# Second attention: four points' stacks instead of two shared ones, and another order at a group's border

## The reference

```python
qkv = (x @ w_qkv.T + b_qkv)                     # 16 heads of 8
std_logits = einsum('bhqd,bhkd->bhqk', q, k) * scale
write_lines = exterior(x_prev @ w1_write.T, x @ w2_write.T)   # 6 numbers a head, unit length
read_lines = exterior(x @ w1_read.T, x @ w2_read.T)
incidence = einsum('bqhp,bkhp->bhqk', read_lines, write_lines @ J6)
bias = incidence * decay ** (q - k) * (k < q) * bias_scale
attn = softmax(causal(std_logits + bias))
out = attn @ v @ w_out.T + b_out
x = x + out
```

## Time and profile before

| | us |
|---|---|
| median of 3 runs | 1821.87 |
| lowest, highest run | 1816.07, 1834.79 |
| profiled execution, span | 1776.1 |
| TensorE busy in the span | 1455.7 (82%) |
| VectorE busy | 1274.7 (72%) |
| ScalarE busy | 935.2 (53%) |
| GpSimd busy | 694.1 (39%) |
| DMA queue of SP, share of 16 engines | 28.1% |

### The profile page before, as it was taken

The page is one execution under the profiler, slowest core; times in us unless marked ns, Lnnn a source line. Parts: engine busy times, 40 slices in busy tenths (PEclk is TensorE's granted clock), DMA queues, the critical chain, the costliest instruction groups (busy, mean ns, idle before and its releaser), DMA issues. The chain is left out here.

```text
span 1776.1 us, 37567 instructions
## 1 busy us (share of the span) xinstructions
PE 1455.7 (82%) x11726; PEld 964.8 (54%) x11726; DVE 1274.7 (72%) x3482; ACT 935.2 (53%) x1914; POOL 694.1 (39%) x812
## 2 busy tenths in 40 slices
PE   3999999999999729995378887878888887837993
PEld 1224334333343319994256766666666665627993
DVE  6777888888787435555777879697978786834555
ACT  2577777777775505662435455454545453314561
POOL 3122342633520334554233344444444541233552
PEclk8699999999998969997689999898999998978997
DMA  6211111111110332222544443434344434132225
GB/s 158 66 42 59 47 52 53 61 53 49 49 62 15 128 123 67 73 72 82 164 150 126 126 128 106 131 109 129 112 125 122 130 111 138 38 130 56 71 72 162
DMA packets 122418, 166.37 MB, mean 94 GB/s; under 512 B 21490, under 2 KB 96018, under 8 KB 121586
## 3 DMA queue, kind: packets, MB, share of 16 engines
q1 hardware_dynamic: 113330, 145.69, 28.1%
q0 software_dynamic: 8896, 18.30, 3.0%
HBM read 116.04 MB, written 47.60 MB: 92 GB/s over the span
## 5 line engine op out<-in xcount | busy, mean ns | idle before, releaser
L1124 DVE TENSOR_REDUCE a_M<-a_F 128x1 f32<-128x512 f32 x512 | 325.8, 683 | 90.0 <-PE a_F L1318 88.1
L1025 ACT ACTIVATE L_W<-a_ST 128x512 f32<-128x512 f32 x512 | 276.8, 595 | 89.1 <-PE a_ST L1359 88.3
L2028 ACT ACTIVATE L_W<-c_ST 128x1024 f32<-128x1024 f32 x160 | 163.3, 1021 | 188.4 <-PE c_ST L2408 141.1
L2630 ACT ACTIVATE L_hT<-L_P,L_W1s 128x128 f32<-128x128 f32 x600 | 171.5, 368 | 142.9 <-PE L_P L2711 110.6
L2616 POOL DMA_INDIRECT L_yd<-L_ys,L_di x150 | 163.1, 1087 | 151.6 <-DVE L_ys L2662 147.2
L489 POOL DMA_INDIRECT L_xd<-L_XN,L_place_i x128 | 124.4, 972 | 146.5 <-issue 131.9
L1359 PE MATMUL a_ST<-L_W 74*128 74x512 bf16 x512 | 168.9, 395 | 11.1 <-ACT L_W L1025 6.3
L1318 PE MATMUL a_F<-L_W 72*128 72x512 bf16 x512 | 167.1, 403 | 7.7 <-DVE a_M L1124 6.9
L2702 PE MATMUL L_P<-L_xT,L_W1s 128*128 128x128 f32 x1200 | 161.0, 278 | 0.0
L2711 PE MATMUL L_P<-L_W,L_hT 128*128 x1200 | 159.1, 276 | 0.1
L2407 PE MATMUL c_ST<-ident,c_SD 128*128 128x128 f32 x512 | 149.7, 292 | 5.5 <-ACT L_W L2028 5.5
(11 more groups left out here) (430 smaller groups left out, 3164.9 us busy)
## 6 DMA issues: line engine op xcount, KB each, us to landing
c_QS<-c_q SPq DMA_DIRECT2D x32, 504.0 KB
c_QS<-c_rd SPq DMA_DIRECT2D x32, 378.0 KB
L_xg<-L_xd SPq DMA_DIRECT2D x150, 64.5 KB
L_W<-a_q SPq DMA_DIRECT2D x32, 288.0 KB
L_W<-a_k SPq DMA_DIRECT2D x96, 96.0 KB
L_W<-c_k SPq DMA_DIRECT2D x96, 96.0 KB
L_W<-in_L_w SPq DMA_DIRECT2D x8, 1024.0 KB
c_QI<-c_r SPq DMA_DIRECT2D x32, 216.0 KB
```

The source lines that it names most:

```text
L1025: act.activation(PT[:, j, kk, :], ST[:, kk, :], ACT.Exp).then_inc(sem(exped), 1)
L1124: dve.tensor_reduce(M[:, t, h:h + 1], FB[n % BANKS][:, :], AX_X, ALU.max).then_inc(sem(maxed), 1)
L2028: act.activation(PT[:, j, :, :], ST[:, :, :], ACT.Exp).then_inc(sem(exped), 1)
L2630: act.activation(hT[:, n % 2, f, :], PS[2 + 2 * (n % 2) + f // 2][:, (f % 2) * P:(f % 2 + 1) * P], func, bias=W1s[:, n % WB, F + f:F + f + ...
```

## The change

QI and KI become twice as wide, so that every group has columns of its own, and SP's waits and issues are put in another order: all four points' stacks of the next sequence are issued as soon as the group of the same number has made its logits. At the opening, the points' stacks of groups 2 and 3 are issued before `x_d` is cleared. TensorE makes the logits of head 1 ahead of `turn_values`, VectorE the maxima of head 1 ahead of `attend`, and parts behind these move with them. The spots of `v`, the lines and their middle parts, `at`, `wo` and `r_ranked` move.

```diff
-        QI = sb("QI", [HALF + PAIRS * PAST, QUAD, S], BF16)
-        KI = sb("KI", [HALF + PAIRS * PAST, QUAD, S], BF16)
+        QI = sb("QI", [HALF + PAIRS * PAST, 2 * QUAD, S], BF16)
+        KI = sb("KI", [HALF + PAIRS * PAST, 2 * QUAD, S], BF16)
...
-        LATE = {4: [("v", 0)]}
-        LATE.update({10 + n: [("line", n)] for n in range(5)})
-        TAIL = {1: [("at", 0)], 2: [("wo", 0)]}
+        LATE = {6: [("v", 0)]}
+        LATE.update({9 + n: [("line", n)] for n in range(5)})
+        TAIL = {3: [("at", 0)], 4: [("wo", 0)]}
         ROUTE = {15: [("r_turned", 0)], 18: [("r_logits", 0)]}
-        RANK = {6: [("r_ranked", 0)]}
+        RANK = {8: [("r_ranked", 0)]}
         CHOICES = {(3, 1): 'cd', (3, 2): 'e', (3, 3): 'f'}
-        MIDS, LMIDS = {24: 0, 25: 1}, {12 + n: n for n in range(5)}
+        MIDS, LMIDS = {24: 0, 25: 1}, {11 + n: n for n in range(5)}
...
             def stack_points(n, g):
                 rows = slice(HALF * (g % 2), HALF * (g % 2) + PAIRS * PAST)
-                stack_left(sp, QI[rows, :, :], r_d, iced[g], QUAD * g)
-                stack_right(sp, KI[rows, :, :], w_d, iced[g], QUAD * g)
+                at = slice(QUAD * (g // 2), QUAD * (g // 2) + QUAD)
+                stack_left(sp, QI[rows, at, :], r_d, iced[g], QUAD * g)
+                stack_right(sp, KI[rows, at, :], w_d, iced[g], QUAD * g)
...
             for g in range(1, NQ):
                 stack_qk(0, g)
                 stack_lines(0, g)
+            for g in range(2, NQ):
+                stack_points(0, g)
             sp.wait_ge(blanked, 2)
             sp.dma_start(r.x_d.rearrange("(e r) c -> r e c", e=E1)[0:P], blank).then_inc(cleared, 16)
-            quad_logits(0, 0)
-            stack_points(0, 2)
 
             def run(i, tail, n1, n2, routed, prev):
                 if n1:
                     store_qk(i + 1)
                     quad_scored(i, 0)
                     stack_qk(i + 1, 0)
-                quad_logits(i, 1)
-                stack_points(i, 3)
                 if n1:
                     store_lines(i + 1)
                     lines_stored(i + 1, 0)
-                    quad_logits(i, 2)
+                    quad_logits(i, 0)
                     stack_points(i + 1, 0)
                     lines_stored(i + 1, 1)
                     stack_lines(i + 1, 0)
+                    quad_logits(i, 1)
+                    stack_points(i + 1, 1)
                     for g in range(1, NQ):
-                        if g == NQ - 1:
-                            quad_logits(i, 3)
-                            stack_points(i + 1, 1)
+                        if g < NQ - 1:
+                            quad_logits(i, g + 1)
+                            stack_points(i + 1, g + 1)
                         quad_scored(i, g)
                         stack_qk(i + 1, g)
                         stack_lines(i + 1, g)
-                    quad_logits(i + 1, 0)
-                    stack_points(i + 1, 2)
...
# VectorE, run():
                 for g in range(NQ):
-                    if g:
-                        attend(i, g - 1)
-                    elif tail:
-                        attend(i - 1, NQ - 1)
-                    if g == 1 and tail:
-                        route_measure(i - 1)
-                    if g == 2 and n2:
-                        measure(i + 2)
                     for j in range(1, QUAD):
                         if has_quad(g, 1, n1):
                             b, q = next_quad(i, g)
                             maxima(b, QUAD * q + j)
-                        if (g, j) == (0, 1) and tail:
+                        if j == 1 and g:
+                            attend(i, g - 1)
+                        elif j == 1 and tail:
+                            attend(i - 1, NQ - 1)
+                        if (g, j) == (1, 1) and tail:
+                            route_measure(i - 1)
+                        if (g, j) == (2, 1) and n2:
+                            measure(i + 2)
+                        if (g, j) == (0, 2) and tail:
                             add_tokens(i - 1)
                         if (g, j) == (0, 1) and n1:
                             sums(i + 1, 1)
-                        if (g, j) == (0, 2) and n1:
+                        if (g, j) == (0, 3) and n1:
                             values(i + 1)
-                        if (g, j) == (0, 3) and routed:
+                        if (g, j) == (1, 1) and routed:
                             r.choose(dve, i - 2, "g", PV)
-                        if (g, j) == (1, 1) and routed:
+                        if (g, j) == (1, 2) and routed:
                             r.choose(dve, i - 2, "h", PV)
...
-                        if (g, j) == (2, 1) and n2:
+                        if (g, j) == (2, 2) and n2:
                             scale(i + 2)
...
# TensorE, logits():
-                    last = pe.matmul(INC[:, ts], QI[rows, h % QUAD, ts], KI[rows, h % QUAD, ts], start=True, stop=True)
+                    at = QUAD * (g // 2) + h % QUAD
+                    last = pe.matmul(INC[:, ts], QI[rows, at, ts], KI[rows, at, ts], start=True, stop=True)
...
# TensorE, run():
                         scores(i, g, j)
+                        spot(g, 2 * j)
+                        if j < QUAD - 1 and has_quad(g, 1, n1):
+                            b, q = next_quad(i, g)
+                            logits(b, QUAD * q + j + 1)
                         if j == 0 and g:
                             turn_values(i, g - 1)
                         elif j == 0 and tail:
                             turn_values(i - 1, NQ - 1)
-                        spot(g, 2 * j)
-                        if j < QUAD - 1 and has_quad(g, 1, n1):
-                            b, q = next_quad(i, g)
-                            logits(b, QUAD * q + j + 1)
```

## The result

The changed kernel took 1856.6 us (1854.4 to 1864.6, four runs) where the kernel before took 1821.8: ratio 1.0201, 95% interval 1.0153 to 1.0248. The forecast was 1812, its range 1797 to 1837. It was wrong, in sign too.

A forecast was written before the change was run, and what follows sets the result against it. No engine bounds the turn alone: VectorE sets groups 0 and 1, TensorE late group 2 and group 3, with a chain between groups. 22 + 10 + 6.5 - 26 - 3 = 9.5 us less: 1812 us, range 1797 to 1837.

The forecast's parts named there:

- B: Points' stacks: own columns in QI and KI end TensorE's waits for them in group 3; 10 us gained (5 to 12).
- C: Order at the groups' border on TensorE and VectorE: 6.5 us gained (2 to 8).
- E: Opening: two points' stacks ahead of clearing x_d delay the first exponentials; 3 us lost (nothing to 5.5).
- A: Lines' chain: lines one spot ahead shorten TensorE's waits before the next batch's logits in group 2; 22 us gained (12 to 24).
- D: Group 1, turns 2 to 6: line 0 waits for routing part g; 5 x 5.2 = 26 us lost (16.5 to 32.5).
- 3.1 + 1.65: Within D: second maxima and part h 3.1 us late, plus 1.65 us if TensorE's clock falls to half for 3.3.
- 5 x 0.6 + 7 x 0.5 = 6.5: C's sum: small savings at the borders of groups 0 and 2, group 3 counted as 0.
- 8.8 + 3.3, less 2 ...: 10: B's sum: 8.8 us of waits and 3.3 of half clock, less 2 that TensorE would wait for the maxima anyway.
- so that costs nothing: Points' stack issues, 3 us each, between group 0's line stack and group 1's stacks were taken as covered, otherwise 6 us.
- slower rival: Lines start behind the wait in spot 9 of group 1, so A is nothing; 19 us more, 1841, chance 0.15.

The follow-up runs named there:

- x_lines_back: x_rank_back with the lines and their middle parts moved back one spot later, where the kernel before had them; 1786.9 us, 1.0057 of the kernel before.
- x_rank_back: Changed kernel with the ranking product in spot 7, routing part g ending group 0, part h first in group 1; 1765.5 us, 0.9925 of the kernel before.
- x_points_late: Changed kernel with points' stacks of groups 1 to 3 issued behind the same group's query, key and line stacks; 1798.8 us, 1.0147 of the kernel before.
- x_border: x_lines_back with SP's order of before as well, leaving the border order and later spots; 1784.8 us, 1.0041 of the kernel before.
- x_points_only: The kernel before with only wider QI and KI, order of issues as before; 1777.2 us, 1.0001 of the kernel before.
- x_measure_first: x_rank_back with x_d cleared before the points' stacks, route_measure before the second head's maxima, route_scale right behind attend; 1751.5 us, 0.9867 of the kernel before.

## Why the prediction was wrong

**The steps that failed are the gains of B and C.** x_lines_back has B, C and E without A and D. By the prediction it is 10 + 6.5 - 3 = 13.5 us faster than before; it was 10 us slower (2 to 18). A and D came out near their terms.

**D, the wait, was right in kind and place and a little too small.** VectorE and GpSimd in group 1 of turn 3, changed kernel, second profile:

```profile
1191.28 0.16 DVE L468 TENSOR_TENSOR L_cursor<-L_cursor,c_PV 128x8 f32<-128x8 f32 x1
1196.15 0.69 DVE L2141 TENSOR_TENSOR c_inc<-c_INC,c_table 128x512 f32<-128x512 f32 x1 [4.72 <-PE c_INC L2376]
...
1200.32 0.91 DVE L473 CAST L_place_i<-L_place 128x8 int32<-128x8 f32 x1
...
1202.63 4.55 DVE L371 TENSOR_SCALAR L_XN<-X,L_rmv,L_rrstd 128x256 f32<-128x256 f32 x4
1207.10 0.68 DVE L2141 TENSOR_TENSOR c_inc<-c_INC,c_table 128x512 f32<-128x512 f32 x1
```

```profile
1202.62 1.15 POOL L1652 TENSOR_TENSOR c_part<-c_rem,c_part 96x512 bf16<-96x512 f32 x1
1203.91 1.15 POOL L1646 TENSOR_TENSOR c_rem<-c_raw,c_part 96x512 f32<-96x512 f32 x1
1205.02 1.20 POOL L1652 TENSOR_TENSOR c_part<-c_rem,c_part 96x512 bf16<-96x512 f32 x1
1206.37 0.66 POOL L1646 TENSOR_TENSOR c_rem<-c_raw,c_part 96x256 f32<-96x256 f32 x1
```

The idle before the second maxima is 4.72 us, above the 2.5 to 4 foretold, because TensorE does the work behind its wait at half clock (granted 0.50 from 1191.6 to 1196.2):

```profile
1191.59 1.06 PE L2337 MATMUL c_PV<-ident,c_line 128*96 128x128 f32 x4 [3.99 <-DVE L_cursor L468]
...
1195.46 0.60 PE L2376 MATMUL c_INC<-c_KI,c_QI 54*128 54x128 bf16 x4
```

(0.60 and 0.39 at full clock.) From part g's end (1191.44) to the maxima it is 4.7 us where I had 2.6, so 2.1 for the clock, near my 1.65. The third maxima stand 21.3 us behind the group's first exponential, against 13.0 in the second profile of before. Of these 8.3 us, 3.05 are the later second maxima, 2.7 part h, now behind them, and 2.3 the scaling, 4.55 us instead of 2.21. The first two are D's, 5.75 where I had 3.1 + 1.65. The last one is neither a wait nor the clock, since GpSimd's parts of the lines now run without a gap beside it, and it is hardly D's: x_rank_back, without the wait, has 4.2 us a turn there. It belongs to C.

```profile
L371 DVE TENSOR_SCALAR L_XN<-X,L_rmv,L_rrstd x20: 409/1338/1383, 1109.9 to 1446.2; 128x256 f32<-128x256 f32 x20
```

A scaling instruction takes 0.40 us alone and up to 1.38 here, and the GpSimd operation beside it 1.15 to 1.20: as I read it, it stands until that one is done. The maxima's first step, which reads one operand from PSUM, takes 0.69 in both kernels. The Trainium skill (SBUF — State Buffer, Who interferes with whom) says that GpSimd and VectorE share a pair of ports as an exclusive lock, which VectorE needs in its two-port modes or with two SBUF inputs, and that the later one waits for the whole instruction. This trace agrees, in the numbers just given. For all of D, 29 us (1.0089 less 0.9925) to 33 us (x_points_late less x_rank_back) were measured, against 26 with a high end of 32.5.

**C, the border, failed in its sum, "5 x 0.6 + 7 x 0.5 = 6.5", which gives group 1 nothing.** Groups 0 and 2 went as expected or better (18.6 from 19.2 in the changed kernel; 21.8 from 23.3 and more in x_border). Group 1, at 24.2 to 24.5 us in the four kernels with this border and without the wait, is longer by 0.7 to 1.8 us than in the profiles of before (x_points_only, with the order of before, comes near it with 23.8). As I read it, that is because route_measure, and with it GpSimd's root and all its line parts behind that root in its queue, come one head step later and meet the scaling, which takes 4.1 to 4.2 us in most turns instead of 2.2. I counted VectorE's instructions with their durations of before, as if these did not depend on what GpSimd does. That it explains all of group 1 is not shown: x_measure_first takes the 2 us back and wins 0.8 there, with other steps long instead. C is 6.5 to 13 us of the gap, as its loss is real or not.

**B failed at "8.8 + 3.3, less 2 ...: 10".** The waits for the points went, as said, but in the other four profiles with the order of before all waits for them are 5.9 to 7.8 us, not 11.3 as in mine (with the 8.8 of rows 5), and some 5 us of waiting come back before the next sequence's first logits: 24.3 against 19.5 on average, and 19.0 against 14.0 in the pair x_lines_back and x_border. That nets 3 to 6 us of waits, and no gain in time: with E, +5 us (-4 to +15) instead of -7. The prediction says of the moved SP issues "so that costs nothing"; the waits grow where they stand, but whether by the transfers behind the line stack or by something else stays open.

**E** was on the path with about 5 us, the high end of its range; I took 3.

**A was right**: 23 us against 22. The chain of the last middle part did move ahead of its reader, though GpSimd still waits as long for that part:

```profile
1247.44 0.67 POOL L1652 TENSOR_TENSOR c_part<-c_rem,c_part 96x256 bf16<-96x256 f32 x1 [4.78 <-ACT c_part L1971]
```

(first profile; the earlier trace rows had 4.24). It ends 3.7 us ahead of group 2's first exponential (1251.85); before, it ended behind the turned values that open the group.

Sum as measured in ratios: -23 (A) +5 (B, E) +7 (C) +29 to 33 (D) = 18 to 22 us more; 16 to 21 were measured. The four terms are not as sure as their sum looks: those of B with E and of C have intervals of 19 and 14 us. The slower rival had the size (19 more) by luck, for its mechanism is wrong: A was not lost.

**The other 15 us of the first measurement** are in group 2. Three engines in turn 3 of its profile:

```profile
1264.08 0.31 PE L2408 MATMUL c_ST<-c_less,c_pick 128*128 128x128 bf16 x1
...
1265.38 0.39 PE L2376 MATMUL c_INC<-c_KI,c_QI 54*128 54x128 bf16 x4
```

```profile
1270.85 1.02 ACT L2027 ACTIVATE L_W<-c_ST 128x1024 f32<-128x1024 f32 x1 [7.85 <-remote]
```

```profile
1270.95 0.69 DVE L2141 TENSOR_TENSOR c_inc<-c_INC,c_table 128x512 f32<-128x512 f32 x1 [6.03 <-DMA L_xd<-L_W]
```

TensorE has done the last block's scores by 1264.4 and the product by 1265.8. The two readers start together at 1270.9, released by names that fit neither. This is so in all of turns 2 to 6, with GpSimd's indirect writes and SP's stacks under way at once, and in none of three later profiles of the same kernel. It makes group 2 longer by 6.4 us on average of turns 2 to 5, and turn 6 by some 9 across the border of groups 1 and 2, 35 us in all, of which the ratio shows only 15; whether the kernel before has part of it on that chip too, no profile shows. Another 33 to 43 us of this slow execution lie ahead of the change: its first exponentials come at 957.6 us, those of the later profiles at 914.9 to 924.2.

## What to carry to other kernels

Ask of each moved piece what will then run beside it, not only what waits for it: a VectorE instruction of 0.40 us became 1.3 because GpSimd's work slid under it. A wait that is taken away may come back at the next one: price the path behind it, and not the wait alone. When a bank's order is written out, look up whose reader the new neighbour is before moving a piece by one spot; here that single step cost some 30 us and hid a gain of 13. And compare a profile with the timed runs of its own chip before taking their difference for something around the span.

## What was not expected of the hardware

- Chips can differ by more than the change: the same kernel took 1822 us on one, on one occasion, and 1773 to 1779 on three others.
- Even VectorE's smallest steps can take the time of a GpSimd instruction that they meet: L477, on 128x4 elements, 1.15 us instead of 0.17.
- In one execution ScalarE and VectorE began 5 to 6 us after TensorE's work was done by the profile, in the same stretch of five turns. The cause is not known.
